# Transposing the normalised FFN input with TensorE and a ScalarE copy in place of a DMA transpose

## The reference

```python
h = shift_token(x)                                   # second half of the features comes from the row before
q, k, v = split(h @ wqkv)                            # 8 heads of 64
q, k = rotary_xpos(l2norm(q) * qs, l2norm(k) * ksc)
x = x + local_attention(q, k, v) @ wo                # windows of 128 rows, each looks at itself and the one before
h = shift_token(x)
h = (h - h.mean(-1)) / sqrt(h.var(-1) + 1e-05) * lg + lb
a, g = split(h @ w1 + b1)                            # 2 * 682 columns
x = x + (a * gelu(g)) @ w2 + b2
```

## Time and profile before

| what | value |
| --- | --- |
| median of 3 runs | 3227.13 us |
| time of the profiled execution | 3229.98 us |
| its span, first to last instruction | 3228.2 us |
| PE busy | 3079.6 us (95%) |
| DVE busy | 2731.2 us (85%) |
| ACT busy | 1945.7 us (60%) |
| POOL busy | 1872.1 us (58%) |
| mean granted TensorE clock | 0.979 |

### The profile page before, as it was taken

One profiled execution on the slowest core, in us unless ns is written; L12 is line 12 of the kernel. 1 busy time (PEld: TensorE's weight loads), 2 busy tenths in 40 slices (PEclk: granted clock), 3 DMA queues, 4 the chain that ended last, 5 costly groups with the idle time before them and its releaser, 6 DMA issues.

```text
span 3228.2 us, 86154 instructions
## 1 busy us (share of the span) xinstructions
PE 3079.6 (95%) x25112; PEld 2590.6 (80%) x25112; DVE 2731.2 (85%) x7864; ACT 1945.7 (60%) x4381; POOL 1872.1 (58%) x2307
## 2 busy tenths in 40 slices
PE   6999999994599999999999999999999999999997
PEld 3675848484488888888888888888888888888886
DVE  6878797875688888888888888899999999999995
ACT  5526181622366676666766666666666667676673
POOL 2333434243566666666666666666767767676763
PEclk9999999996799999999999999999999999999999
DMA  1111202015111111111111111122121121211211
GB/s 37 40 59 31 73 19 72 26 63 199 51 45 51 55 49 50 47 53 51 51 49 48 53 49 54 49 52 66 54 61 54 56 64 56 59 54 56 66 56 44
DMA packets 275103, 179.35 MB, mean 56 GB/s; under 512 B 95278, under 2 KB 272914, under 8 KB 274578
## 3 DMA queue, kind: packets, MB, share of 16 engines
q1 hardware_dynamic: 274962, 177.86, 19.0%
HBM read 106.44 MB, written 54.54 MB: 50 GB/s over the span
## 4 chain that ended last, share of the span: by engine, by line
PE 71%; DVE 1%; POOL 1%; issue 1%; ACT 0%; DMA 0%; POOLq 0%; DVEq 0%; SPq 0%; ACTq 0%
PE b_ps L867 16%; PE b_ps L942 14%; PE b_ps L953 10%; PE b_ps L895 7%; PE b_ps L883 7%; PE b_ps L921 6%; PE b_ps L908 6%; PE b_ps L852 2%; PE b_ps L845 2%; PE b_ps L834 1%; POOL b_sq L1188 0%; POOL b_rn L1221 0%; DVE b_probs L1136 0%; DVE b_probs L1149 0%; POOL b_t L1210 0%
## 5 line engine op out<-in xcount | busy, mean ns | idle before, releaser
L1000 ACT ACTIVATE b_probs<-b_probs,b_negmax 128x256 f32<-128x256 f32 x1024 | 505.9, 495 | 78.3 <-DVE b_negmax L1136 77.4
L867 PE MATMUL b_ps<-b_wqkv,b_hT_hi 128*128 128x512 f32 x1536 | 494.5, 403 | 1.0 <-DVE b_hT_lo L1024 1.0
L942 PE MATMUL b_ps<-b_h2T,b_w 128*128 128x256 f16 x4224 | 474.0, 273 | 6.5 <-DMA b_h2T<-b_xh_hl 6.5
L942 PEld LDWEIGHTS b_ps<-b_h2T,b_w 128*128 128x128 f16 x4224 | 414.3, 98 | 55.2 <-DMA b_h2T<-b_xh_hl 6.9
L1188 POOL TENSOR_TENSOR b_sq<-b_sq 128x512 f32<-128x512 f32 (+5 forms) x768 | 418.7, 545 | 61.7 <-ACT b_sq L981 21.6
L1221 POOL TENSOR_TENSOR b_rn<-b_ss_min,b_mhalf 128x16 f32<-128x16 f32 x128 | 377.4, 2948 | 108.8 <-DVE b_ss_min L1048 108.6
L1149 DVE TENSOR_SCALAR b_probs<-b_probs,b_rinv 128x256 f32<-128x256 f32 x1024 | 409.6, 442 | 18.2
L1198 POOL TENSOR_TENSOR b_rstd<-b_var,b_mhalf 128x1 f32<-128x1 f32 x128 | 72.0, 562 | 555.8 <-DVE b_var L1109 555.8
L442 PE MATMUL a_ps<-a_xs,a_E 128*128 128x256 f16 x3072 | 345.2, 273 | 4.1 <-POOL a_xs L233 4.0
L953 PE MATMUL b_ps<-b_w,b_hid 128*128 128x256 f32 x1536 | 342.2, 379 | 1.2 <-DVE b_hid L1172 1.2
L434 PE MATMUL a_ps<-a_xnT 128*128 128x512 f16 x1536 | 339.2, 385 | 3.0 <-ACT a_xnT L382 2.4
(11 more groups left out here) (133 smaller groups left out, 6507.5 us busy)
## 6 DMA issues: line engine op xcount, KB each, us to landing
b_hx<-xs_dram SPq DMA_DIRECT2D x256, 64.0 KB, 1.9
b_rot<-rot_dram SPq DMA_DIRECT2D x128, 128.0 KB, 2.1
b_xr<-xs_dram SPq DMA_DIRECT2D x128, 128.0 KB, 2.1
xp_dram<-b_xp SPq DMA_DIRECT2D x128, 128.0 KB, 1.7
b_h<-xp_dram SPq DMA_DIRECT2D x256, 64.0 KB, 1.8
a_xn<-in_L_attn_x_dram SPq DMA_DIRECT2D x20, 512.0 KB, 3.8
a_x_res<-in_L_attn_x_dram SPq DMA_DIRECT2D x66, 128.0 KB, 2.1
x_dram<-a_x SPq DMA_DIRECT2D x64, 128.0 KB, 1.7
```

What stands on the lines that cost most here:

```text
L867: last = nc.tensor.matmul(ps[:, bank, :], hT[:, k, :], wqkv[:, ds(layer(s), 1), part, k, bank * INNER:(bank + 1) * INNER], start=(k == 0 a ...
L942: last = nc.tensor.matmul(ps[:, bank, half * 2 * P:(half + 1) * 2 * P], w1[:, ds(layer(2 * j), 1), wp, k, first:first + P], h2T[:, hp, k, ...
L1000: nc.scalar.activation(probs[:, h, :], probs[:, h, :], ACT.Exp, bias=negmax[:, h:h + 1], scale=-1.0, accum_out=rowsum[:, h:h + 1]).then_in ...
```

## The change

The DMA transpose leaves SyncE's list. In its place TensorE transposes the four 128x128 f16 pieces of `xh_hl` in each slot, between the scores (L908) and `wo` (L921), into the first half of PSUM bank 7, and ScalarE copies the 128x512 f16 result into `h2T`, in front of the first exp (`H2T_AT = 0`). An f16 identity is made once, in the preparation. The waits follow: the transposes wait for both parts of `xh_hl` and for `oT_lo`, the transposes of hx wait for ScalarE's copy (`h2T_kept`) where they waited for `oT_lo`, the w1 product waits for the copy, and DVE's and POOL's waits on the DMA become one wait of DVE on the transposes.

```diff
-                    t = s - 3
-                    if in_range(t):
-                        wait_apart(sp, xh_hi, t + 1, passed_sp)
-                        wait_apart(sp, xh_lo, t + 1, passed_sp)
-                        if r % 2 == 1:
-                            wait_apart(sp, w1_done, HC * (pairs - 1), passed_sp)
-                        wait_apart(sp, h2T_loaded, 16 * t, passed_sp)
-                        n = (r - 3) % 2
-                        sp.dma_start_transpose(h2T[:, :, :, n * P:(n + 1) * P].rearrange("p a k n -> p (a k) n"),
-                                               xh_hl[:].rearrange("p a d -> p (a d)")).then_inc(h2T_loaded, 16)
...
                 def transpose_hx(t, r):
                     pe.wait_ge(hx_loaded, 32 * (t + 1))
-                    wait(pe, oT_lo, t - 2)
+                    wait(pe, h2T_kept, t - 3)
...
+                def transpose_h2(t):
+
+                    if in_range(t):
+                        pe.wait_ge(xh_hi, t + 1)
+                        pe.wait_ge(xh_lo, t + 1)
+                        if in_range(t + 1):
+                            pe.wait_ge(oT_lo, t + 2)
+                        else:
+                            pe.wait_ge(h2T_kept, t)
+                        for part in range(2):
+                            for k in range(KD):
+                                last = nc.tensor.transpose(ps_h2T[:, part, k, :], xh_hl[:, part, k * P:(k + 1) * P], ident_h[:])
+                        last.then_inc(h2T_done, 1)
...
                             if p % 2 == 1:
                                 last.then_inc(scores_done, 1)
+                    transpose_h2(s - 3)
                     t = s - 2
...
-                        pe.wait_ge(h2T_loaded, 16 * (2 * j + 2))
+                        pe.wait_ge(h2T_kept, 2 * j + 2)
...
+                def keep_h2T(t, r, pairs):
+                    if in_range(t):
+                        act.wait_ge(h2T_done, t + 1)
+                        if r % 2 == 1:
+                            wait(act, w1_done, HC * (pairs - 1))
+                        n = (r - 3) % 2
+                        nc.scalar.copy(h2T[:, :, :, n * P:(n + 1) * P], ps_h2T).then_inc(h2T_kept, 1)
...
                         for p in range(HP):
+                            if p == H2T_AT:
+                                keep_h2T(s - 3, r, pairs)
                             for h in range(2 * p, 2 * p + 2):
                                 act.wait_ge(scores_kept, HEADS * t + h + 1)
                                 nc.scalar.activation(probs[:, h, :], probs[:, h, :], ACT.Exp, bias=negmax[:, h:h + 1], scale=-1.0,
                                                      accum_out=rowsum[:, h:h + 1]).then_inc(exp_done, 1)
...
-                        wait(dve, h2T_loaded, 16 * t)
+                        wait(dve, h2T_done, t)
...
                         pool.wait_ge(xh_hi, t + 1)
-                        wait(pool, h2T_loaded, 16 * t)
```

More of the change, by code:

```diff
@@ L47 @@
 EVEN_MASK, ODD_MASK = 3, 4
+H2T_AT = 0
 XS_SCALE = 2.0 ** 9
@@ L523, in phase_b @@
         mask = sb("mask", [P, 5, 2 * P], BF16)
-        ident_f = sb("ident_f", [P, P])
+        ident_f, ident_h = sb("ident_f", [P, P]), sb("ident_h", [P, P], F16)
         mhalf = sb("mhalf", [P, 2 * HEADS])
@@ L673, in _ @@
                 dve.wait_ge(loaded, 16 * DMAS)
+                nc.vector.tensor_copy(ident_h[:], ident_f[:])
                 nc.vector.tensor_copy(mask[:], mask_f[:])
@@ L739, in phase_b @@
             st2_ready, mv2_ready, var2_ready, rstd2_ready = (sem(n) for n in ("st2_ready", "mv2_ready", "var2_ready", "rstd2_ready"))
-            xh_ready, xh_hi, xh_lo, h2T_loaded = (sem(n) for n in ("xh_ready", "xh_hi", "xh_lo", "h2T_loaded"))
+            xh_ready, xh_hi, xh_lo, h2T_done, h2T_kept = (sem(n) for n in ("xh_ready", "xh_hi", "xh_lo", "h2T_done", "h2T_kept"))
             w1_done, gelu_done, hid_ready = sem("w1_done"), sem("gelu_done"), sem("hid_ready")
@@ L744, in phase_b @@
             rstdf_ready, xf_ready, fin_ready = sem("rstdf_ready"), sem("xf_ready"), sem("fin_ready")
+            ps_h2T = ps[:, 7, 0:D].bitcast(F16).rearrange("p (a k n) -> p a k n", a=2, k=KD)
             vk_cleared = sem("vk_cleared")
@@ L888, in run @@
                         if not in_range(s):
-                            pe.wait_ge(oT_lo, t)
+                            pe.wait_ge(h2T_kept, s - 3)
                         for p in range(HP):
```

## The result

The changed kernel takes 3270.19 us (median of 4 runs, 3269.72 to 3274.61), the kernel before 3227.84 us beside it (4 runs). The ratio is 1.0134, with a 95% interval of 1.0116 to 1.0151: slower, by 42 us. The profiled executions have spans of 3269.2 and 3228.2 us, 41.0 us apart.

The account below looks back on a forecast made before the run. TensorE was taken to bound phase B; transposes 29 us, late DVE in 12 slots 5 and drain 0 summed to 34 us, giving 3261 us on the 3227.13 us median, with a range of 3242 to 3290 us.

Parts of the forecast that it names:

- What bounds the kernel: Phase B: TensorE is the limit, busy 2107.3 of 2120 us, so work added to its stream lengthens the run.
- the removed part: DMA transposes: removing them gains nothing outside the drain, as TensorE waited for them only once, for 6.5 us.
- The transposes: TensorE, between scores and L921: four f16 transposes cost 0.23 us in each of 128 slots, 29 us, bounds 19 to 56.
- ScalarE: Copy in front of the exps: exps 0.9 us late in even slots, 2.03 in odd ones behind an exposed table load.
- the rival of a dearer load: Odd slots: a second 1.28 us at each table switch adds 51 us on top of 34, 3312 us; chance 0.01.
- hT_lo: DVE makes it by 2031.9 or 2032.5, just in time for TensorE's L867 at 2032.67; no cost counted.
- DVE becomes the limit: Rival: TensorE waits at L867 or L1088, 29 us on top of the transposes' 29, 3285 us; chance 0.09.
- The 12 slots behind a jump: Layer 1's even slots beginning a loop iteration: late DVE costs TensorE 0.4 us each at L1088, 5 us, bounds 0 to 10.
- The drain: Last slots: h2T about 1.2 us quicker, once, against DVE about a microsecond later; clock stays low; counted as zero.
- The sum: Whole kernel: 29 + 5 + 0 = 34 us, giving 3261 us on the median, 1.05% slower.

Follow-up runs that it names:

- the transposes alone: The kernel before, DMA transpose kept, with four f16 transposes added on TensorE that nobody reads: 3250.15 us, ratio 1.0069.
- the last run: The changed kernel with ScalarE's copy of the transposed h2 one step later, behind the first pair of exps: 3291.85 us, ratio 1.0195.
- the early load: The changed kernel with a one-column exp ahead of ScalarE's copy in odd slots, loading the exp table earlier: 3246.86 us, ratio 1.0057.
- the copy alone: The kernel before, DMA transpose kept, with ScalarE's copy out of bank 7 to an unread tile and its waits: 3244.56 us, ratio 1.0050.
- the fourth run: The changed kernel with SyncE waiting for qT_hi before the h2 loads in layer 1's last slot of each iteration: 3271.55 us, ratio 1.0130.

## Why the prediction was right, and where it was not

**What bounds the kernel, and the removed part: right.** TensorE is the limit in both kernels, and in 1100 to 3190 us of before no wait for the DMA transpose existed that could be won.

**The transposes: right in mechanism, somewhat dear.** Predicted 0.23 us x 128 = 29 us from phase A's row; measured 0.20 to 0.21 us from the first transpose to L929, and 0.02 to 0.03 us given back in L929's own length: 25.2 - 3.0 = 22.2 us in the changed kernel and 22.5 in the kernel with the transposes alone. I had asked what they hide in front of them, where the row said 0.21 us before and says 0.21 us after, and not what they change behind them. The Trainium skill (VectorE: DVE Perf Modes, "The three transpose paths") gives 390 ns for a 128x128 transpose on TensorE and 1309 ns by DMA, and its section "Rules for kernel authors" advises TensorE where a PSUM destination will do. No run here shows 390 ns: the record of one f16 transpose is 0.22 us, and four in a stream cost 0.18 us together. Nor does one show the 1309 ns by itself: the DMA's record of 1.2 us is that of all four pieces, and they landed 2.48 us after the issue. And the advice led the wrong way, since the 1.2 us of the DMA lay beside TensorE's work and the 0.18 us of TensorE do not.

**ScalarE: right.** The order copy, table load, exp came as forecast, and the exps were 1.93 us late in odd slots for 2.03. In even slots they were 0.67 late for 0.9, since the copy starts 0.44 us after the first transpose and not 0.55. No drain appears beside the exposed table load (2038.01 + 1.28 = 2039.29, exp at 2039.31), so the rival of a dearer load is out: 0.02 us, not 1.28. The gelus lost nothing, and the hx transposes never waited for the copy (the last run shows how near that was: an exp pair of about a microsecond).

**hT_lo: nearly right.** I had it "just in time". It is late by 4.5/64 = 0.07 us in an average even slot: at the jump above it ends at 2229.44 and L874 starts 0.85 us into the slot for 0.79 before. That makes 4.5 us, not 0 and not the 19 of the rival in which DVE becomes the limit.

**The 12 slots behind a jump: the step that failed.** Predicted 12 x 0.4 = 5 us, bounds 0 to 10, at the subtraction of `oT` (L1088). Measured 17.1 + 0.9 = 18 us, at the v product. Two errors, one of reading and one of assumption. I asked where DVE's slack lies at the end of the chain and took L1088, far downstream, and did not ask who is the first to wait for the instruction right behind the pause: `qT_low` frees the bank of the v product, with 0.41 us of slack. And I took the pause of 1.35 us as fixed. It is not: it was 1.20 to 1.35 with DVE 0.44 us behind TensorE, 1.21 to 1.55 with the early load, and 1.9 to 2.5 where DVE is 0.8 to 1.3 us behind.

What hardly changes is the time from DVE's last reciprocal to `qT_low`. DVE ahead of the jump, before and after:

```profile
2213.45 0.15 DVE L1146 RECIPROCAL b_rinv<-b_rowsum 128x2 f32<-128x2 f32 x1
2213.64 1.35 DVE L1149 TENSOR_SCALAR b_probs<-b_probs,b_rinv 128x256 f32<-128x256 f32 x2
...
2229.36 0.15 DVE L1166 RECIPROCAL b_rinv<-b_rowsum 128x2 f32<-128x2 f32 x1
2229.54 0.62 DVE L1169 TENSOR_SCALAR b_probs<-b_probs,b_rinv 128x256 f32<-128x256 f32 x2
```

From the end of that reciprocal to the start of `qT_low` are 3.25 to 3.39 us at the 12 jumps before and 3.36 to 3.78 after, in the mean 3.29 and 3.56; with the copy alone, where the pause is 2.1 us, they are 3.41, and with the early load, where it is 1.4, they are 3.41 too. So most of the longer pause is no new loss. Before, the last two scalings took 1.35 us, as they do beside POOL's L1232 in the earlier trace rows, and filled that time; after, DVE comes later, they take 0.62, and the 0.73 us turn up as pause. The true lateness is that of the reciprocal: it ended 0.88 us ahead of TensorE's slot before and 0.69 us into it after, 1.57 us later, where my 0.3 to 0.8 us looked at the end of the scalings (measured 0.81). 1.57 + 0.27, less the slack of 0.41, are 1.4 us, which is the 17.1 us of the 12 slots.

**The drain: 3.0 us gained, not 0.** The quicker way of h2T gave 1.5 us, for 1.2 forecast: from the end of the lower part of `xh_hl` to the last w1 product are 1.16 us, for 2.65 before. The clock gave 2.4 us; I had written that it stays low there, and below is what it did. The longer wait for DVE took back 0.4 us, and two more sets of transposes 0.5.

**The sum.** Predicted +34 us, measured +41 on the profiled spans and +42 on the medians: +18 for 5 at the jumps and +4.5 for 0 at hT_lo, less 7 at the transposes and 3 in the drain. The time of 3261 us missed by 9, and the miss is smaller than the error of 13 us in its largest wrong term only because two other terms erred the other way. That is luck, and so are the 2.4 us that the clock gave in the drain (below). Of the rivals, "DVE becomes the limit" was nearest in kind: its wait exists, but it is tied to the jumps.

**What stays open:** why the fetch hangs on the reciprocal. On the queue q14 "instruction" packets of 8 KB move near each jump, the first between the reciprocal and `qT_low`, and another about 2.5 us later at most of them. The first starts 1.38 us after the end of the reciprocal before (mean of 12) and 1.63 us after, and `qT_low` starts 1.9 us behind it in both. With the h2 loads moved (the fourth run) the 1.63 us are 1.41, which is the 0.2 us of traffic. The reciprocal is the last of DVE's own results for which its list waits ahead of the jump, so I take it that DVE's sequencer can't go on to the jump before it. That fits the traces of all nine kernels (3.25 to 3.78 us from the reciprocal to `qT_low` wherever a packet moved), but it is argued and not shown: no run moved the reciprocal.

## What to carry to other kernels

Before moving work off a DMA queue, ask whether the transfer is ever waited for; if not, there is nothing to win there, and what moves to the engine that is the limit is paid in full (here 0.18 us in each slot), with a gain only where nothing covers the transfer (here the drain). An instruction put in front of a table load can expose the load (here 1.28 us, 23 us in all): look at what stands in the idle time in front of the place and not only at what the new instruction takes; a tiny activation ahead of it gives the cover back. Where the trace shows a pause at regular places, find the first wait behind it and its slack, and measure the pause from the last result that the engine had to wait for and not from its last instruction.

## What the runs showed of the hardware

**Jumps back and instruction packets.** In layer 0's loops (1050 to 2150 us) DVE shows no pause at the jump, and the queue q14 moves 9 packets; in layer 1's loop (2170 to 3190 us) it moves 68, and each jump has its pause. The two windows of the DMA view, the changed kernel (queue, packets, MB, share):

```profile
q14 instruction: 9, 0.07, 0.0%
...
q14 instruction: 68, 0.56, 0.2%
```

The Trainium skill (Runtime: NRT & Kernel Launch, "Instruction fetch mechanics") says that a taken branch to code outside the window that the engine holds forces a fetch before the engine can go on. The trace agrees, with 1.2 to 2.5 us of pause behind a jump in layer 1, where packets move, and none in layer 0. That the queue's packets belong to DVE I infer from their times alone.

**The clock after a short wait.** Before, TensorE stood idle for 2.25 us and the sixteen transposes behind took 3.51 us. The window around them has a granted clock of 0.57 (columns as in the earlier trace rows):

```profile
3168.00:3172.00 4.00, 3.60 (x18) 3.43 (x20) 1.72 (x7) 1.80 (x4) 1.23 (x2) 0.57 0.54 168
```

After, the window of the same place has 1.00:

```profile
3212.00:3216.00 4.00, 3.10 (x38) 2.94 (x40) 2.22 (x8) 2.05 (x4) 1.56 (x3) 1.00 0.57 165
```

And the timeline of PE in the last slots, after:

```profile
3212.91 1.97 PE L890 MATMUL b_ps<-b_ident_f,b_probs 128*128 128x128 f32 x16 [2.68 <-DVE b_xpp L1081]
...
3244.95 0.38 PE L841 MATMUL b_ps<-b_ident_h,b_xh_hl 128*128 128x128 f16 x4 [3.90 <-DVE b_xh_hl L1138]
3246.01 8.95 PE L950 MATMUL b_ps<-b_h2T,b_w 128*128 128x256 f16 x66 [0.68 <-ACT b_h2T L981]
```

The same sixteen transposes took 1.97 us behind a wait of 2.68 us, at the fast level, 2.4 GHz, where before they fell to 1.2 GHz behind a wait of 2.25 us. The length of the wait does not decide, and neither does the change. The same place in the changed kernel with the h2 loads moved, and in the one with the transposes alone:

```profile
3213.07 3.53 PE L892 MATMUL b_ps<-b_ident_f,b_probs 128*128 128x128 f32 x16 [2.68 <-DVE b_xpp L1083]
...
3188.48 1.97 PE L897 MATMUL b_ps<-b_ident_f,b_probs 128*128 128x128 f32 x16 [2.23 <-DVE b_xpp L1076]
```

A wait of 2.68 us was followed by either level, and so was one of 2.23 to 2.25 us. What tells them apart no run here shows. With the last w1 product, 8.95 us for 9.85, the clock gave 1.54 + 0.90 = 2.4 us of the drain's gain, in the one profiled execution of each kernel; it can't be put down to the change.
